# A Mamba-style layer with a mixture of experts on eight cores: small state operations moved to VectorE, gate blocks moved beside the scan, tail weights in four parts

## The reference, cut to what matters

```python
x_and_res = x @ W_in
xi, res = jnp.split(x_and_res, 2, axis=-1)
xi = silu(causal_conv4(xi, conv_w) + conv_b)
BC = xi @ W_xproj                      # 16 B and 16 C values per row
delta = softplus(xi @ W_dt + b_dt)
A = -jnp.exp(A_log)
def step(h, inp):                      # over the 4096 rows
    u_i, d_i, B_i, C_i = inp
    dA = jnp.exp(d_i[:, None, :] * A[None, :, None])
    h = h * dA + d_i[:, None, :] * B_i[:, :, None] * u_i[:, None, :]
    y_i = jnp.sum(h * C_i[:, :, None], axis=1)
    return (h, y_i)
y = (ys + xi * D_param) * silu(res)
x = layernorm(x + y @ W_out)
# then: top 2 of 16 experts by softmax scores, plus two shared experts
x = layernorm(x + x + routed + shared)
```

## Time and profile before

| what | us |
|---|---|
| time, median of 3 runs | 3603.54 |
| lowest and highest run | 3592.22, 3635.76 |
| the profiled execution | 3598.11 |
| its longest span (core 3, SECOND) | 3596.5 |
| core 3: VectorE, GpSimd, ScalarE, TensorE busy | 2798.2, 2841.3, 2077.7, 2075.9 |
| core 3: first scan at, prefix ends at, own chunks end at | 111.9, 1987.5, 3128.8 |
| core 4 (FIRST): first scan at, chunks end at, span | 155.7, 2822.5, 3579.4 |

### The profile page before, as it was taken

One profiled execution on the slowest core, in us unless ns is written; L12 is line 12 of the kernel. 1 busy time (PEld: TensorE's weight loads), 2 busy tenths in 40 slices (PEclk: granted clock), 3 DMA queues, 4 the chain that ended last, 5 costly groups with the idle time before them and its releaser, 6 DMA issues.

```text
span 3596.5 us, 50310 instructions; the slowest of 8 cores (3546.1 to 3596.5 us)
## 1 busy us (share of the span) xinstructions
PE 2075.9 (58%) x10828; PEld 1263.4 (35%) x10828; DVE 2798.2 (78%) x1664; ACT 2077.7 (58%) x4666; POOL 2841.3 (79%) x1548
## 2 busy tenths in 40 slices
PE   3356444444444353535434878888788786686760
PEld 2234323233322232323322545445354442242330
DVE  1579888798978887979788899898998999853214
ACT  2467767767666666767666655656556555320114
POOL 0689999999998999999999888797887888502002
PEclk8677767676767676767677889899899998897885
DMA  7655345574868586768684525233253233014875
GB/s 168 164 147 169 106 138 145 134 176 122 220 175 158 113 195 111 190 122 183 129 173 114 143 57 158 86 110 131 57 153 97 74 83 119 34 48 140 298 257 194
DMA packets 161244, 502.87 MB, mean 140 GB/s; under 512 B 20426, under 2 KB 80586, under 8 KB 138082
## 3 DMA queue, kind: packets, MB, share of 16 engines
q1 hardware_dynamic: 130962, 376.55, 34.3%
q0 software_dynamic: 29968, 122.92, 18.1%
HBM read 516.14 MB, written 123.47 MB: 178 GB/s over the span
## 4 chain that ended last, share of the span: by engine, by line
DVE 28%; issue 21%; PE 15%; DMA 14%; POOL 10%; ACT 7%; SPq 1%; another core or an unknown queue 1%; DVEq 1%; ACTq 0%; POOLq 0%
DVE hb L1083 13%; DVE PP L1083 12%; POOL hb L614 9%; DMA RA<-wbd 6%; PE PP L817 4%; PE PP L832 4%; DMA r<-xs 3%; PE PP L1357 2%; DMA RA<-wbc 2%; DVE hb L1089 2%; PE PP L1248 2%; ACT PP L947 1%; PE PP L787 1%; DMA RA<-W_inx 1%; SPq L673 1%
## 5 line engine op out<-in xcount | busy, mean ns | idle before, releaser
L614 POOL TENSOR_TENSOR hb<-du,bcl 128x1020 f32<-128x1020 f32 x1024 | 2370.2, 2347 | 89.1 <-PE PP L832 67.2
L1083 DVE TENSOR_TENSOR_SCAN hb<-PP,hb 128x1024 f32<-128x1024 f32 x764 | 1711.9, 2278 | 333.3 <-ACT hb L967 188.4
L947 ACT ACTIVATE PP<-dring,negA 128x1020 f32<-128x1020 f32 x1024 | 1125.0, 1099 | 2.6 <-issue 2.2
L817 PE MATMUL PP<-xib,RA 128*128 128x256 bf16 x4096 | 590.7, 310 | 460.1 <-DMA RA<-wbd 199.8
L832 PE MATMUL PP<-hb,sid 128*128 128x512 f32 x1280 | 635.6, 635 | 146.1 <-ACT PP L981 63.3
L817 PEld LDWEIGHTS PP<-xib,RA 128*128 128x128 bf16 x4096 | 441.3, 110 | 636.1 <-issue 540.5
L1083 DVE TENSOR_TENSOR_SCAN PP<-PP,hb 128x1024 f32<-128x1024 f32 x260 | 594.4, 2286 | 35.4 <-ACT hb L967 32.0
L787 PE MATMUL PP<-xb,RA 128*128 128x256 bf16 x2688 | 408.7, 318 | 70.8 <-ACT sres L896 34.5
L960 ACT ACTIVATE carry<-hb 128x4 f32<-128x4 f32 x764 | 157.3, 206 | 490.1 <-DVE hb L1083 485.9
L799 PE MATMUL PP<-xiraw,RA 128*128 128x256 bf16 x1024 | 181.3, 336 | 437.8 <-ACT xiraw L866 373.4
L832 PEld LDWEIGHTS PP<-hb,sid 128*128 128x128 f32 x1280 | 244.0, 205 | 417.3 <-issue 414.1
(11 more groups left out here) (156 smaller groups left out, 1464.0 us busy)
## 6 DMA issues: line engine op xcount, KB each, us to landing
RA<-wbd SPq DMA_DIRECT2D x120, 1024.0 KB, 6.8
RA<-wbx SPq DMA_DIRECT2D x160, 512.0 KB, 4.6
wre<-Wre POOLq DMA_DIRECT2D x16, 2048.0 KB, 20.0
RA<-wbc SPq DMA_DIRECT2D x120, 256.0 KB, 3.5
bcl<-bc_hbm SPq DMA_DIRECT2D x176, 128.0 KB, 8.6
bcl<-bc_hbm SPq DMA_DIRECT2D x80, 256.0 KB, 6.1
ys<-r SPq DMA_DIRECT2D x32, 512.0 KB, 10.0
xs<-zb SPq DMA_DIRECT2D x50, 256.0 KB, 5.3
```

The lines of the kernel that those rows point to most:

```text
L614: ge.tensor_tensor(ct3(hb[st % NB][:])[:, :, 1:TA], ct3(du[q % 2][:])[:, :, 1:TA], bcl[n][:, 1:TA].rearrange("p (o t) -> p o t", o=1) .bro ...
L817: mm = te.matmul(b[:, 0:TA], wdt[j % NDT][:, (c * CT + q) * 128:(c * CT + q + 1) * 128], xib[:, q * TA:(q + 1) * TA], start=(q == 0), stop ...
L947: se.activation(out=ct3(dec[b])[:, :, 1:TA], in_=ct3(d_of(q))[:, :, 1:TA], func=AF.Exp, scale=negA[:, n:n + 1]).then_inc(s_dA, 1)
L1083: ve.tensor_tensor_scan(out=hout, data0=dec[b], data1=hb[st % NB][:], initial=0.0, op0=ALU.mult, op1=ALU.add).then_inc(s_scan, 1)
```

## The change

Three edits.

1. On SECOND, for the 44 quarters of the prefix, the zt product and the three operations of carry_in are issued by VectorE (prefix_z, prefix_carry) in place of GpSimd. GpSimd keeps du. prefix_z(q + 1) stands ahead of scan n = 6 (11 in chunk 0), prefix_carry(q + 1) ahead of scan n = 12 (14 in chunk 0), and each with the waits it had.
2. On FIRST, the eight gate blocks of chunk 0 move from the pass k = -1 to the steps 1, 2, 5, 6, 9, 10, 11 and 13 of chunk 0 (RS0), the casts of their weights 3 to 7 to steps 2, 3, 6, 7 and 10 of GpSimd (RS0_CAST), and the four SiLUs to steps 14 and 27 of ScalarE. load_x(1) is issued ahead of the first three of those casts.
3. On FIRST, each DMA of the tail weights becomes four of 32 partitions each, at n = 1, 5, 9 and 13 (PARTS = 4). SECOND keeps one.

```diff
@@ -334,6 +334,7 @@
         NQ, NR0, NS = 4 * NK, PK * NSTEP, NK * NSTEP
         DOFF = (2 - 4 * (NK - 1)) % ND
         T0 = PK * TA
+        PARTS = 4 if PK == 0 else 1
         JT = RB // 128
         NCLR = (NBLK + NBLK - NFIX) * JT
         NSP = max(0, NT - NBAS)
@@ -349,6 +350,9 @@
             return k >= PK
 
         LATE = {4: 3, 5: 4, 6: 7, 7: 8, 8: 18, 9: 19, 10: 23, 11: 24, 12: 34, 13: 35, 14: 39, 15: 40}
+
+        RS0 = (1, 2, 5, 6, 9, 10, 11, 13)
+        RS0_CAST = {2: 3, 3: 4, 6: 5, 7: 6, 10: 7}
 
         def shift(k):
 
@@ -388,8 +392,8 @@
                         out.append(("dt", k + 1, c))
             if k >= 1 and is_real(k) and s % 3 == 1 and s < 24:
                 out.append(("rs", k, s // 3))
-            if k < 0 and is_real(0) and s >= 46 and s % 2 == 0 and s < 62:
-                out.append(("rs", 0, (s - 46) // 2))
+            if k == 0 and is_real(0) and s in RS0:
+                out.append(("rs", 0, RS0.index(s)))
             return out
 
         def weight_of(key):
@@ -533,6 +537,10 @@
                     ge.wait_ge(s_hc, q - 1)
                 ge.tensor_tensor(du[q % 2][:], d_of(q), quarter(u_b[(k + NK) % 2], qd),
                                  ALU.mult).then_inc(s_du, 1)
+                if q < 4 * PK:
+                    return
+                if q >= 1:
+                    ge.wait_ge(s_z, q)
                 d0 = ct3(d_of(q))[:, :, 0:1].rearrange("p c o -> p o c")
                 ge.tensor_tensor(nc4(zt[q % 2][:]), d0.broadcast_to([128, NST, QC]),
                                  negA[:].rearrange("p (n o) -> p n o", o=1).broadcast_to([128, NST, QC]),
@@ -558,21 +566,23 @@
                     ge.wait_ge(s_pad, NST * (q - 1))
                 ge.tensor_tensor(hc[q % 2][:], zt[q % 2][:], wt[:], ALU.add).then_inc(s_hc, 1)
 
-            def tail_weights(i):
+            def tail_weights(i, part):
+
+                w = slice(part * (128 // PARTS), (part + 1) * (128 // PARTS))
                 if i == 0:
-                    ge.dma_start(out=wob, in_=W_outx).then_inc(s_wob, 16)
+                    ge.dma_start(out=wob[w], in_=W_outx[w]).then_inc(s_wob, 16)
                 if i == 1:
-                    ge.dma_start(out=wst, in_=Wsx[0]).then_inc(s_ws, 16)
+                    ge.dma_start(out=wst[w], in_=Wsx[0][w]).then_inc(s_ws, 16)
                 if i == 3:
-                    ge.wait_ge(s_ws, 16)
-                    ge.dma_start(out=wst.rearrange("p (a c) -> (p a) c", c=D),
-                                 in_=Wsx[1].rearrange("p (a c) -> (p a) c", c=D),
+                    ge.wait_ge(s_ws, 16 * PARTS)
+                    ge.dma_start(out=wst[w].rearrange("p (a c) -> (p a) c", c=D),
+                                 in_=Wsx[1][w].rearrange("p (a c) -> (p a) c", c=D),
                                  accum_op=ALU.add, max_dma_last_dim=4096).then_inc(s_ws, 16)
                 if i == 5:
-                    ge.wait_ge(s_ws, 32)
-                    ge.dma_start(out=wsb, in_=wst).then_inc(s_ws, 16)
+                    ge.wait_ge(s_ws, 32 * PARTS)
+                    ge.dma_start(out=wsb[w], in_=wst[w]).then_inc(s_ws, 16)
                 if 6 <= i < 6 + NEXP:
-                    ge.dma_start(out=wre[i - 6], in_=Wre[i - 6]).then_inc(s_wre, 16)
+                    ge.dma_start(out=wre[i - 6][w], in_=Wre[i - 6][w]).then_inc(s_wre, 16)
 
             ge.dma_start(out=wxp[:], in_=W_xp).then_inc(s_wxp, 16)
             cast_weights(("xi", 0, 0))
@@ -586,18 +596,22 @@
             if PK == 0:
                 cast_u(0, 0)
                 cast_u(0, 1)
-                for p in range(8):
+            load_x(1)
+            if PK == 0:
+                for p in range(3):
                     cast_weights(("rs", 0, p))
-            load_x(1)
             ge.wait_ge(s_negA, 1)
             ge.wait_ge(s_init, 6)
             prepare(0)
-            carry_in(0)
+            if PK == 0:
+                carry_in(0)
             for st in range(NS):
                 k, s = st // NSTEP, st % NSTEP
                 q, n = st // NST, st % NST
                 if k == 0 and s in (0, 1, 12, 13, 28, 29):
                     cast_weights(("dt", 0, {0: 4, 1: 6, 12: 8, 13: 10, 28: 12, 29: 14}[s]))
+                if PK == 0 and k == 0 and s in RS0_CAST:
+                    cast_weights(("rs", 0, RS0_CAST[s]))
                 if k == 2 and s == 2:
                     ge.dma_start(out=tri[:], in_=tri128).then_inc(s_k0, 16)
                     ge.dma_start(out=scent[:].rearrange("p (k n) -> p k n", n=NEXP),
@@ -616,12 +630,12 @@
                                  .broadcast_to([128, QC, TA - 1]), ALU.mult).then_inc(s_dbu, 1)
                 if st - LAG >= NR0 and on_pool(st - LAG - NR0):
                     product(st - LAG)
-                if n == 5:
-                    tail_weights(q - cut.QT)
+                if n % 4 == 1 and n // 4 < PARTS:
+                    tail_weights(q - cut.QT, n // 4)
                 if q + 1 < NQ:
                     if n == (11 if k == 0 else 6):
                         prepare(q + 1)
-                    if n == 15:
+                    if n == 15 and q + 1 >= 4 * PK:
                         carry_in(q + 1)
             for st in range(NS - LAG, NS):
                 if on_pool(st - NR0):
@@ -743,7 +757,7 @@
                 if k == NK - 1 and s == 40:
                     sy.wait_ge(s_mm, len(USE))
                     sy.wait_ge(s_ev, len(USE))
-                    sy.wait_ge(s_wob, 16)
+                    sy.wait_ge(s_wob, 16 * PARTS)
                     sy.dma_start(out=wout, in_=wob).then_inc(s_wol, 16)
                     sy.wait_ge(s_dA, NS - NSTEP)
                     sy.wait_ge(s_z, NQ - 4)
@@ -999,12 +1013,9 @@
                     for half in range(2):
                         if s == (13 if half == 0 and k + 1 >= PK else 26) + shift(k):
                             silu_u(k + 1, half)
-                if k == -1 and is_real(0) and s == NSTEP - 1:
-                    for qd in range(4):
-                        silu_res(0, qd)
-                if k >= 1 and is_real(k):
+                if k >= 0 and is_real(k):
                     for half in range(2):
-                        if s == (13, 26)[half]:
+                        if s == ((14, 27) if k == 0 else (13, 26))[half]:
                             silu_res(k, 2 * half)
                             silu_res(k, 2 * half + 1)
 
@@ -1071,10 +1082,51 @@
                     ve.wait_ge(s_zt, 48)
                 ve.tensor_tensor(g_b[r % 2][:], YB, quarter(sres, qd), ALU.mult).then_inc(s_g, 1)
 
+            def prefix_z(q):
+
+                ve.wait_ge(s_d, q + 1)
+                if q >= 2:
+                    ve.wait_ge(s_hc, q - 1)
+                d0 = ct3(d_of(q))[:, :, 0:1].rearrange("p c o -> p o c")
+                ve.tensor_tensor(nc4(zt[q % 2][:]), d0.broadcast_to([128, NST, QC]),
+                                 negA[:].rearrange("p (n o) -> p n o", o=1).broadcast_to([128, NST, QC]),
+                                 ALU.mult).then_inc(s_z, 1)
+
+            def prefix_carry(q):
+
+                k, qd = q // 4, q % 4
+                ve.wait_ge(s_e, q + 1)
+                if q >= 4:
+                    ve.wait_ge(s_car, NST * (q - 3))
+                ve.wait_ge(s_b0[k % 2], 16 * (k // 2 + 1))
+                ve.wait_ge(s_du, q + 1)
+                if q >= 1:
+                    ve.wait_ge(s_hc, q)
+                w = slice(qd * NST * QC, (qd + 1) * NST * QC)
+                du0 = ct3(du[q % 2][:])[:, :, 0:1].rearrange("p c o -> p o c")
+                ve.tensor_tensor(zt[q % 2][:], zt[q % 2][:], carry[:, w], ALU.mult).then_inc(s_pb, 1)
+                ve.tensor_tensor(nc4(wt[:]), du0.broadcast_to([128, NST, QC]),
+                                 b0t[k % 2][:].rearrange("p (n o) -> p n o", o=1)
+                                 .broadcast_to([128, NST, QC]), ALU.mult).then_inc(s_pb, 1)
+                ve.wait_ge(s_pb, 2 * (q + 1))
+                if q >= 2:
+                    ve.wait_ge(s_pad, NST * (q - 1))
+                ve.tensor_tensor(hc[q % 2][:], zt[q % 2][:], wt[:], ALU.add).then_inc(s_hc, 1)
+
+            if PK > 0:
+                ve.wait_ge(s_negA, 1)
+                ve.wait_ge(s_init, 6)
+                prefix_z(0)
+                prefix_carry(0)
             for st in range(NS):
                 k, q, n = st // NSTEP, st // NST, st % NST
                 r = st - NR0
                 b = decay_slot(st)
+                if q + 1 < 4 * PK:
+                    if n == (11 if k == 0 else 6):
+                        prefix_z(q + 1)
+                    if n == (14 if k == 0 else 12):
+                        prefix_carry(q + 1)
                 ve.wait_ge(s_dbu, st + 1)
                 ve.wait_ge(s_dA, st + 1)
                 ve.wait_ge(s_pad, st + 1)
@@ -1126,7 +1178,7 @@
                 ).then_inc(s_wl[b % 3], 16)
 
             ge.wait_ge(s_op, NT)
-            ge.wait_ge(s_wre, 16 * NEXP)
```

(3 more changed lines are left out.)

## The result

The changed kernel takes 3740.7 us (median of 4 runs, 3736.5 to 3808.0) where the kernel before takes 3598.3 beside it: ratio 1.0385, 95% interval 1.0336 to 1.0433. It is slower by 142 us, and 174 us slower than predicted. In some executions of most kernels one die (four of the cores) shows a lower granted clock and the time is some per cent longer; ratios, and the times given for the experiments, leave these out, and of e3, which has no other, only the undisturbed die of core 3 is read.

What follows compares the result with a forecast made beforehand. Core 3 of SECOND sets the time, with GpSimd the bound in its prefix. Gains of 22 us (chunks 1 to 4), 5 (chunks 5 to 10) and 4 (chunk 0) sum to 31: 3598.1 - 31 = 3567 us, range 3533 to 3598.

Steps and rivals of the forecast that it cites:

- The bound and its margin: SECOND's prefix, chunks 1 to 4: GpSimd stays the bound at 39.2 us a quarter, VectorE needs 38.5, margin 0.7.
- the nearest row is the router's operation ... I take four times 0.22, 0.9 us a quarter: SECOND's prefix: price of the four moved operations on VectorE, read from a 226 ns router row.
- The upper bound of 1.5: SECOND's prefix: most the moved operations could cost VectorE per quarter, GpSimd's own 1.37 us rounded up.
- GpSimd's relief: SECOND's prefix: GpSimd loses 1.37 us a quarter, all of it arriving in chunks 1 to 4 as 22 us.
- rival C: SECOND's prefix: scans stand behind prefix_carry waiting for ScalarE's exp; 2.5 us of wait gives 3663; chance 0.05.
- Rival B: SECOND's chunks 5 to 10: weights set the pace, VectorE's gain becomes waits for ScalarE; 11 us gained, 3587; chance 0.14.
- Chunks 5 to 10: SECOND's prefix: ScalarE's 133.8 us of VectorE waits stay; VectorE pays 21.6, gets 24.7 back; gain taken as 5 us.
- What follows the prefix: Core 3's own chunks and tail were taken as fixed in length.
- Part two: FIRST's chunk 0: first product 41 us earlier, 8 us given back by the added work, net 33.
- a rival of 68 us: FIRST's chunk 0: five casts each wait 13.5 us for a store, FIRST becomes the bound, 3608; chance 0.03.
- Part three: FIRST's chunks 2 to 6: smaller tail-weight transfers delay weight loads less; 44 us, half of 88.
- FIRST's end: FIRST cores end at 3502 us, or 3546 without the split tail weights, both before SECOND's 3565.5.

Runs made afterwards that it cites:

- e3: Kernel before, plus four-part tail weights on FIRST and five unused VectorE operations per SECOND prefix quarter; core 3's chunks 5 to 10 took 1144.6 us against 1022.7.
- e4: Changed kernel with GpSimd made to stand still in the prefix while VectorE does the moved operations; 3649.7 us, ratio 1.0149 to before.
- e7: Changed kernel with GpSimd held to two products ahead of the scan in the prefix; 3837.3 us, one execution.
- e9: Changed kernel with two of the four small prefix operations on ScalarE and two back on GpSimd, second run; 3569.2 us, ratio 0.991 to before.
- e2: Changed kernel with the tail weights on FIRST back to one whole DMA; 3785.9 us, one run.
- e8: Kernel of e9 with the gate blocks of chunk 0 on FIRST moved back ahead of the scan; ratio 0.9875 to before.
- e1: Changed kernel with the four small prefix operations back on GpSimd, the FIRST edits kept; 3580.5 us, ratio 0.9952 to before.

## Why the prediction was wrong, step by step

**The bound and its margin: right as read, and the reason the error was so dear.** GpSimd did set the pace, and in the prediction's sum VectorE was only 0.7 us a quarter behind it once the operations were moved. With so thin a margin VectorE's waits are all that can take up an error in its price: they took up 155 of 331 us, and the rest came through.

**The step that failed: "the nearest row is the router's operation ... I take four times 0.22, 0.9 us a quarter".** The row has the same engine, type and size, and e4 shows that its 0.22 to 0.25 is right for an idle GpSimd. But in chunks 1 to 10 of the prefix GpSimd is busy for 97 to 99% of the time, and the row's condition was not looked at. Measured: 8.5 us a quarter (373.5 / 44). The upper bound of 1.5 failed for the same reason: it was built from how long the operation runs, and held no case in which it can't start. The trace of before had no VectorE operation with all inputs in SBUF beside a busy GpSimd: in its prefix VectorE does nothing but scans, one input in PSUM. That gap was the thing to price, with a wait for one GpSimd product, 2.34 us, as the next row at hand; four of those a quarter would have given 9.4 us, near the 8.5 that came, though with luck in it: 41 of the 176 did not wait at all and 34 waited through more than one product.

**GpSimd's relief: right.** It lost the four operations' time, and in chunks 1 to 4 its busy time fell by 17.1 us and its own wait ahead of the state sum, 3.6, went with them: 21 of the 22 expected. GpSimd then stood idle there for 90.7 us, waiting for buffers.

**The waits of VectorE in line (rival C): fell.** In the prefix after the first scan VectorE waited 13.2 us for softplus and 7.9 once for a carry; for the exp of zt there is no wait among its groups. The sign was C's, but neither the mechanism nor the size: C with its 2.5 us of wait has 3663, 78 us below what came.

**Rival B's sum.** Its 22 + 0 - 11 = 11 belongs to operations of 1.5 us a quarter (24.7 - 36 = -11). For the 0.9 that it names first it would be 22 - 21.6, nothing, and 3598. That changes no verdict here.

**Chunks 5 to 10: wrong in kind.** ScalarE's 133.8 us of waits, which were taken as fixed, shrank to 57.4. They were in part slack, as I read it: a slower VectorE finds its first columns ready. That, with GpSimd's lead, is the 155 us of idle time that covered the other half of the 331.

**What follows the prefix: not fixed.** The own chunks kept their length (3 us less), the tail of core 3 fell from 467.7 to 437.0. Its expert blocks, first and last copy of each kernel (before, after):

```profile
L1677 DVE COPY r<-PP x32: 1224/1225/1226, 3325.1 to 3513.8; 128x1024 f32<-128x1024 f32 x32
```

```profile
L1729 DVE COPY r<-PP x32: 1224/1225/1226, 3492.0 to 3659.7; 128x1024 f32<-128x1024 f32 x32
```

188.7 us became 167.7. In the table of core 3 the tail is 447 to 470 us where the prefix is fast and 430 to 445 where it is slow. Before, cores 2 and 4 of FIRST were at their expert blocks until 3396 and 3419, so the two kinds of cores loaded expert weights at the same time for 70 to 95 us; after the change they end at 3350, and core 3 begins at 3492. That would shorten the tail if two cores' loads slow each other. It is argued from these times, not shown by a run of its own, and single cores go against it: core 7 takes 192.2 us for its expert blocks in e7, where FIRST has ended its own over 200 us before, and 164.7 in e9, where the two overlap. If it holds, a part of each microsecond won in the prefix is given back.

**Part two: its start right, its price too low.** First scan of core 4 at 118.4, expected about 114. The stops of the five casts were named, with a bound of 41 and a rival of 68 us, and then priced at 8; they cost 24.7 on GpSimd's queue, and chunk 0 28. Of the 33 us net that were worked out, 9 were left at the end of chunk 0.

**Part three: right in kind, a little better than taken.** Chunks 2 to 6 of core 4 fell from 1265.0 to 1208.7, 56 us where 44 was taken. Of it e2 gives 33 us to the parts themselves; e8, with part three and without part two, has 42 us for the mean of the cores. By the row of the Trainium skill that the prediction names (DMA: Bandwidth & Descriptors, Rules for kernel authors) parts bring nothing. That was not borne out here: what counted was not the transfer's own time but TensorE's waits for its weights, 111.8 us in e2 and 74.3 with the parts.

**FIRST's end: right, with luck.** 3508.1 us where 3502 was worked out. Part two gave 9 us instead of 33 at the end of chunk 0, and part three 56 instead of 44; the rest came from the tail of core 4, which was 9 us shorter (756.9 to 747.6) and was taken as fixed.

**e1 as a test of the rest.** Without part one core 3 needed 3581.7 us, 15 below before (10 in the mean of the four SECOND cores), which the prediction had at nothing. The earlier place of SECOND's DMA issue and the earlier end of FIRST are both in it. Had the operations cost what I took, the forecast's 31 us would have come on top of that; no run shows this, since in none did VectorE do them without either a wait or a stop of GpSimd.

## What to carry to other kernels

Before moving small operations from a busy GpSimd to VectorE, look where their inputs lie: in these traces each one with all of them in SBUF waits for the end of GpSimd's instruction, and if it misses that end, until GpSimd stands still; with one in PSUM it doesn't, and ScalarE doesn't either. A price read from a trace is a price under the conditions of its row, so note what the neighbouring engine did at that time. And where two engines are within a few per cent of each other, a bound on an unknown wait has to ask what happens if the operation can't start, not only how long it runs.

## What the runs showed of the hardware that I had not expected

- A VectorE operation on 128x64 f32 with both inputs in SBUF ended 0.08 to 0.09 us after a GpSimd instruction, after waits of up to 13.66 us over six products in a row; GpSimd's product kept its 2.34 us throughout. With one input in PSUM: 190 to 193 ns in 44 of 44 cases.
- It gets in at the first end of a GpSimd instruction or, if it misses that one, not before GpSimd stands still. Of the 135 waiting operations of core 3, 101 ended at the first end, 79 of them between two back-to-back instructions (recorded 30 to 70 ns over each other), after 0.67 to 2.39 us. The 34 others all ended where GpSimd then stood still for 2.7 us or more, and none at a gap in between. On the other three SECOND cores 4 of 104 such waits did end in between. The first probe of e3 has the same two kinds, 23 and 21. What decides whether the first end is taken is not settled.
- Beside an instruction of GpSimd that only issues a DMA it did not wait: 13 operations ran beside one in 225 to 253 ns.
- The length of a chunk hangs on the phase of these waits: SECOND ran chunks 5 to 10 in 1092 or 1136 us, with sums of 373.5 or 434.6 us over the prefix, in two kernels whose SECOND programs differ only in the step at which GpSimd issues one DMA a quarter (the transfers of FIRST differ as well).
